# A gated delta rule kernel: log beta of the source token in the one decay exponent, instead of a second decay matrix

## The reference, cut to what matters

```
beta = sigmoid(hidden @ Wb.T)
g = -exp(A_log) * softplus(hidden @ Wa.T + dt_bias)
def step(S, inp):
    qt, kt, vt, gt, bt = inp
    S = S * exp(gt)                      # decay
    pred = einsum('bhk,bhkv->bhv', kt, S)
    dv = (vt - pred) * bt                # the write is scaled by beta
    S = S + einsum('bhk,bhv->bhkv', kt, dv)
    ot = einsum('bhk,bhkv->bhv', qt, S)
```

## Time and profile before

| | |
|---|---|
| runs | 1966.24, 1972.13, 1974.1 us; median 1972.13 us |
| span of the profiled execution | 1970.6 us (1.5 us less than the median of the runs) |
| TensorE matmul busy | 1809.7 us, 92% |
| VectorE busy | 1601.0 us, 81% |
| ScalarE busy | 1034.9 us, 53% |
| GpSimd busy | 414.1 us, 21% |
| chain that ended last, by engine | TensorE 76%, VectorE 10%, issue 9%, ScalarE 1% |
| TensorE clock, mean share granted | 0.944 |
| DMA | 13 GB/s on average |

### The profile page before, as it was taken

One profiled execution on the slowest core, in us unless ns is written; L12 is line 12 of the kernel. 1 busy time (PEld: TensorE's weight loads), 2 busy tenths in 40 slices (PEclk: granted clock), 3 DMA queues, 4 the chain that ended last, 5 costly groups with the idle time before them and its releaser, 6 DMA issues.

```text
span 1970.6 us, 102023 instructions
## 1 busy us (share of the span) xinstructions
PE 1809.7 (92%) x45376; PEld 1515.8 (77%) x45376; DVE 1601.0 (81%) x4326; ACT 1034.9 (53%) x1999; POOL 414.1 (21%) x325
## 2 busy tenths in 40 slices
PE   4689999999999999999999999999999999998886
PEld 3577787887878787878778877878887887787765
DVE  3777898888888888888988888899888889887631
ACT  3644555555555545555555555555555556554422
POOL 0212122222212222221222222122122221221200
PEclk8878999999999999999999999999999999998766
DMA  3000000000000000000000000000000000000000
GB/s 102 1 3 3 14 14 14 4 14 14 14 14 14 9 9 14 14 14 15 14 5 12 14 14 14 14 14 10 7 14 14 14 9 9 9 4 9 8 8 12
DMA packets 21447, 26.26 MB, mean 13 GB/s; under 512 B 2193, under 2 KB 20753, under 8 KB 21009
## 3 DMA queue, kind: packets, MB, share of 16 engines
q1 hardware_dynamic: 21008, 19.73, 3.0%
HBM read 11.33 MB, written 8.39 MB: 10 GB/s over the span
## 4 chain that ended last, share of the span: by engine, by line
PE 76%; DVE 10%; issue 9%; ACT 1%; DVEq 0%; POOL 0%; ACTq 0%; POOLq 0%
PE ps L239 36%; PE ps L221 15%; PE ps L230 9%; PE ps L214 4%; DVE CV L1107 3%; PE ps L411 2%; PE ps L363 2%; PE ps L589 2%; PE ps L579 2%; PE ps L598 2%; PE ps L207 2%; PE ps L381 1%; DVE XR L1384 1%; DVE eg L1364 1%; PE ps L472 1%
## 5 line engine op out<-in xcount | busy, mean ns | idle before, releaser
L1107 DVE SCALAR_TENSOR_TENSOR CV<-ps,cw,CV 128x256 f32<-128x256 f32 x576 | 250.5, 477 | 8.8 <-ACT CV L872 1.9
L239 PEld LDWEIGHTS ps<-QE,S 64*64 64x64 f32 x4096 | 212.4, 140 | 56.7 <-issue 55.2
L239 PE MATMUL ps<-QE,S 64*64 64x16 f32 x4096 | 254.9, 211 | 1.0 <-ACT S L673 1.0
L239 PE MATMUL ps<-WP,V 64*64 64x16 f32 x4096 | 252.5, 210 | 0.0
L239 PEld LDWEIGHTS ps<-WP,V 64*64 64x64 f32 x4096 | 213.4, 140 | 0.0
L239 PE MATMUL ps<-WP,KD 64*64 64x48 f32 x4096 | 144.6, 226 | 28.6 <-issue 26.8
L239 PEld LDWEIGHTS ps<-WP,KD 64*64 64x64 f32 x4096 | 134.4, 141 | 38.7 <-issue 37.4
L1007 POOL TENSOR_TENSOR XK<-XK 128x512 f32<-128x512 f32 x32 | 33.7, 1052 | 608.5 <-ACT XK L846 608.5
L1122 DVE TENSOR_TENSOR prod<-A,TZ 128x30 f32<-128x30 f32 (+7 forms) x480 | 141.4, 295 | 13.2
L239 PEld LDWEIGHTS ps<-SA,M 32*32 32x32 f32 x8192 | 93.2, 109 | 67.3 <-issue 40.5
L221 PE MATMUL ps<-w_r_ffn,XR 128*128 128x256 f32 x512 | 137.6, 416 | 6.7 <-DVE XR L1096 6.7
(11 more groups left out here) (156 smaller groups left out, 4019.8 us busy)
## 6 DMA issues: line engine op xcount, KB each, us to landing
X<-in_x SPq DMA_DIRECT2D x32, 256.0 KB, 2.7
out_x<-X SPq DMA_DIRECT2D x32, 256.0 KB, 2.1
w_r_ffn<-in_wT_r_ffn SPq DMA_DIRECT2D x1, 256.0 KB, 3.3
w_k_ffn<-in_wT_k_ffn SPq DMA_DIRECT2D x1, 256.0 KB, 3.6
w_v_ffn<-in_wT_v_ffn SPq DMA_DIRECT2D x1, 256.0 KB, 4.5
w_k<-in_wT_k SPq DMA_DIRECT2D x1, 256.0 KB, 4.5
w_q<-in_wT_q SPq DMA_DIRECT2D x1, 256.0 KB, 4.8
w_v<-in_wT_v SPq DMA_DIRECT2D x1, 256.0 KB, 5.1
```

The lines of the kernel that those rows point to most:

```text
L239: last = mm(ps[rows, o:o + n], stat[rows, pk].rearrange("p s c -> p (s c)"), mov[rows], **flags)
L1107: last = stt(d4[:, m], src, cw[:, i, m, tap:tap + 1], d4[:, m], ALU.mult, ALU.add)
```

## The change

Log beta of the source token j is put on the diagonal of `ST` before the running sums, so that the one exponent that `decay_steps` gives holds the decay from j to i and log beta of j. The one exponential `E` then carries beta wherever `EA` or `be` carried it:

- TensorE: `beta_in` (four 128x128 by 128x128 multiplications a group) is gone. `decay_steps` closes its sums itself.
- ScalarE: `beta_log` (128x512 copy) and `exp_a` (128x512 exponential) are gone.
- GpSimd: `b_diag` (128x512) is gone. `beta_diag` (128x512 product of -log beta and the diagonal mask, waits for `gb`) is new, and `stat1` has a second instruction, a 128x512 subtraction, that waits for the first one and for `beta_diag`.
- VectorE: `b_reduce` (a reduction of 128x512 and a 128x64 product) is gone. In `t_out0` and `t_out1` the product with `be` becomes a copy, and the product with `be2` becomes one with the mask `slot`; both have the shapes of before. `gram0` to `gram3` read `E` in place of `EA`.
- Waits: those on `ea`, `be`, `lb`, `bd` are gone or turned into waits on `e` and `ld`. The tiles `EA`, `LB`, `be`, `be2` are gone, `LD` is new.

```diff
@@ tensor
-                    last = mm(ps[:, o:o + P], ST[:, c0:c0 + P], cum_i, start=(ub == 0), stop=False, skip_group_check=True)
+                    last = mm(ps[:, o:o + P], ST[:, c0:c0 + P], cum_i, start=True, stop=True)
...
-            def beta_in(g):
-                pe.wait_ge(s["lb"], g + 1)
-                pe.wait_ge(s["e"], g + 1)
-                for ub in range(M * B):
-                    o, c0 = 4 * BANK + ub * P, (ub % B) * NH * C + ub // B * P
-                    last = mm(ps[:, o:o + P], LB[:, c0:c0 + P], ident, start=False, stop=(ub == M * B - 1), skip_group_check=True)
-                last.then_inc(s["ea_ps"], 1)
...
             def gram0(g):
                 pe.wait_ge(s["k_slots"], 4 * g + 4)
                 pe.wait_ge(s["qhat"], g + 1)
-                pe.wait_ge(s["ea"], g + 1)
+                pe.wait_ge(s["e"], g + 1)
@@ scalar
-            def beta_log(g):
-                act.wait_ge(s["gb"], g + 1)
-                if g:
-                    act.wait_ge(s["ea_ps"], g)
-                af(packs(LB[:]), along(cz[:, BH:2 * BH]), ACT.Copy, scale=-1.0).then_inc(s["lb"], 1)
...
-            def exp_a(g):
-                act.wait_ge(s["ea_ps"], g + 1)
-                if g:
-                    act.wait_ge(s["gram_used"], 4 * g)
-                    act.wait_ge(s["bd"], g)
-                af(EA[:], bank(4), ACT.Exp).then_inc(s["ea"], 1)
@@ gpsimd
-            def b_diag(g):
-                pool.wait_ge(s["ea"], g + 1)
-                pool.wait_ge(s["eg"], g + 1)
-                if g:
-                    pool.wait_ge(s["be"], g)
-                tt(packs(BD[:]), packs(EA[:]), over_packs(diag), ALU.mult).then_inc(s["bd"], 1)
...
+            def beta_diag(g):
+                pool.wait_ge(s["gb"], g + 1)
+                tt(packs(LD[:]), along(cz[:, BH:2 * BH]), over_packs(diag), ALU.mult).then_inc(s["ld"], 1)
+
             def stat1(g):
                 pool.wait_ge(s["gb_wide"], g + 1)
                 if g:
                     pool.wait_ge(s["d_ps"], g)
-                tt(packs(ST[:]), packs(GB[:]), vw(after_j, [0, BH], [1, C]), ALU.mult).then_inc(s["stat1"], 1)
+                own.done(tt(packs(ST[:]), packs(GB[:]), vw(after_j, [0, BH], [1, C]), ALU.mult))
+                pool.wait_ge(s["ld"], g + 1)
+                own.settle()
+                tt(ST[:], ST[:], LD[:], ALU.subtract).then_inc(s["stat1"], 1)
...
                 on(square3, g)
                 on(gate_norm, f)
                 on(q_decayed, e)
+                on(beta_diag, d)
                 on(stat1, d)
@@ vector
             def t_out0(g):
                 ve.wait_ge(s["t_ps"], 2 * g + 1)
-                ve.wait_ge(s["be"], g + 1)
...
                 own.done(tt(WP[g % 2][:, rows, 0:U].rearrange("p k (s c) -> p k s c", s=2),
-                            vw(src, [U, C], [0, 2], [1, C]), vw(be2[:, rows], [2, C], [1, 2], [0, C]), ALU.mult))
-                tt(WP[g % 2][:, rows, U:], src[:, :, C:U], along(be[:, rows]), ALU.mult).then_inc(s["wp"], 1)
+                            vw(src, [U, C], [0, 2], [1, C]), vw(slot, [0, C], [1, 2], [0, C]), ALU.mult))
+                nc.vector.tensor_copy(WP[g % 2][:, rows, U:], src[:, :, C:U]).then_inc(s["wp"], 1)
...
-                own.done(tt(packs(AT[:])[:, rows], src[:, :, 0:C], packs(EA[:])[:, rows], ALU.mult))
+                own.done(tt(packs(AT[:])[:, rows], src[:, :, 0:C], packs(E[:])[:, rows], ALU.mult))
...
-            def b_reduce(g):
-                ve.wait_ge(s["bd"], g + 1)
-                if g:
-                    ve.wait_ge(s["wp"], 2 * g)
-                chained(nc.vector.tensor_reduce(be[:], packs(BD[:]), AX_X, ALU.add))
-                tt(be2[:], along(be[:], 2), over_packs(slot), ALU.mult).then_inc(s["be"], 1)
```

More of the change, by code:

```diff
@@ L75, in macaron_kernel @@
         E = sb("E", [P, COLS])
-        EA = sb("EA", [P, COLS])
         EQ = sb("EQ", [P, COLS])
@@ L79, in macaron_kernel @@
         GD = sb("GD", [P, COLS])
-        BD = GD
         GI2 = sb("GI2", [P, PACKS, U])
@@ L84, in macaron_kernel @@
         A4 = sb("A4", [P, COLS])
-        LB = sb("LB", [P, COLS])
+        LD = sb("LD", [P, COLS])
         TZ = sb("TZ", [P, 2, 2, C, C])
@@ L119, in macaron_kernel @@
         names = ("first_in ffn_in mix_in x_in out_stored zeroed setup_act xt1_ps yt_ps xt3_ps k1_ps r1_ps v1_ps k3_ps r3_ps v3_ps "
-                 "q_ps k_ps v_ps g_ps ssk_ps ssq_ps oss_ps wo_ps eq_ps d_ps ea_ps hal1 hal3 haly rstd1 rstd2 rstd3 "
[3 rows of a table removed]
+                 "q_ps k_ps v_ps g_ps ssk_ps ssq_ps oss_ps wo_ps eq_ps d_ps hal1 hal3 haly rstd1 rstd2 rstd3 "
[3 rows of a table added]
                  "tapv gram_ps gram_used t_ps wp kd_ps mt b_ps o_ps ch_ps ch_s k_slots v_slots s_slots act_step "
-                 "vec_step").split()
+                 "vec_step pool_step").split()
         s = {n: sem(n) for n in names}
@@ L528, in ffn3_r @@
                     pe.wait_ge(s["gram_used"], min(4 * g + 9, 4 * GROUPS))
-                    pe.wait_ge(s["ea"], min(g + 3, GROUPS))
+                    pe.wait_ge(s["e"], min(g + 3, GROUPS))
                     pe.wait_ge(s["mt"], min(4 * g + 8, 4 * GROUPS))
@@ L632, in _ @@
                 on(chain, d, 1)
-                on(beta_in, c)
                 on(chain, d, 2)
@@ L943, in _ @@
                 on(norm1, b)
-                on(beta_log, d)
                 on(xt1, b)
@@ L952, in _ @@
                 on(norm3, f)
-                on(exp_a, d)
                 on(relu1, b)
@@ L986, in _ @@
             tt = nc.gpsimd.tensor_tensor
+            own = Steps(pool, s["pool_step"])
             def g_ident(g):
@@ L1053, in _ @@
                 on(g_ident, e)
-                on(b_diag, e)
                 on(square1, c)
@@ L1178, in soft_one @@
                     ve.wait_ge(s["gb"], g)
-                    ve.wait_ge(s["lb"], g)
+                    ve.wait_ge(s["ld"], g)
                 ts(uz[:], ez[:], 1.0, None, ALU.add).then_inc(s["uz"], 1)
@@ L1388, in gram0 @@
                 ve.wait_ge(s["gram_ps"], 4 * g + 1)
-                ve.wait_ge(s["ea"], g + 1)
                 ve.wait_ge(s["em"], g + 1)
@@ L1572, in _ @@
                 on(solve1, d)
-                on(b_reduce, d)
                 on(solve2, d)
```

2 lines of the change are left out of this document (removed), and 6 rows, old and new, of the table names.

## The result

| | before | after |
|---|---|---|
| median of 20 runs | 1972.69 us | 1985.01 us |
| lowest to highest | 1959.9 to 1983.1 | 1967.0 to 2000.5 |
| span of the profiled execution | 1970.6 us | 1987.4 us |
| TensorE clock in it, mean share granted | 0.944 | 0.931 |

The ratio after to before is 1.0064, with a 95% interval of 1.0044 to 1.0083: the kernel became 0.6% slower, where I had forecast 0.3% faster. The page of the kernel after shows what was expected in the busy times (GpSimd up from 414 to 437 us, the others down), and one thing that was not: the clock row.

The account below looks back on a forecast made before the run. TensorE's wait for `norm3` ahead of `turn3` was taken to cover `beta_in`'s saving. Terms 3.5 + 2.0 + 2.3 - 2.3 = 5.5 us less, so span 1965.1 and median 1966.6 us, 0.28% faster; range 1951 to 1990.

Parts of the forecast that it names:

- the one on the clock: New gap of 1.33 us ahead of `turn3`: judged nearer the 1.66 stop without a fall; no clock term in the sum.
- What bounds the kernel: TensorE at `turn3` waits for `norm3`, whose path does not pass through `beta_in`; `turn3` stays, gap grows 0.67 to 1.33.
- the term of 3.5 us: `chain 4` no longer set by VectorE's copy of `chain 3`: gain of 0.14 or 0.15 us in 24 groups.
- Rival A: `beta_in` on TensorE: the whole slot counts, 1.09 us in every group, 35 us gained, 1937 us; chance 0.06.
- Late groups: Groups where TensorE itself reaches `turn3` late: 0.57 us gained in three, 0.24 in a fourth, together 2.0 us.
- first and last groups: Gains of 1.1 us in the first group, 1.0 in the second, 0.2 in the last, together 2.3 us.
- GpSimd and `shift1`: GpSimd's longer work ahead of `stat1` holds `shift1` on VectorE, which ends 0.70 us later, as does `norm1`.
- the term of 2.3 us of loss: `turn1` waits for the later `norm1`: 0.32 us lost in 7 groups and 0.1 in one.
- rival D: VectorE ahead of `norm1`: `beta_diag` holds the statistics of `stats1`, `turn1` waits, 30 us lost, 1997 us; chance 0.08.
- The copies: VectorE's copy replacing the second product of `t_out0`: taken as 0, bounds -0.15 and 0 per copy.
- Rival B: Instructions reach TensorE sooner, relieving supply stops in rows of small instructions: 20 us more gained, 1945 us; chance 0.08.
- Rival C: Wider gap ahead of `turn3` makes TensorE's clock fall, 1.7 us each: 1987 us in half the groups, 2007 in all; chance 0.17.

Follow-up runs that it names:

- turn3_later: The kernel after with `turn3` moved behind `chain 3` and `gram0` on TensorE; 1981.35 us, ratio 1.0038 to the kernel before.
- after_again: The kernel after run once more, nothing changed; 1984.41 us, ratio 1.0050 to the kernel before.
- before_wide_gap: The kernel before, `beta_in` kept, with two extra activations delaying `norm3` to widen the gap ahead of `turn3`; 2011.23 us, ratio 1.0209.

## Why the prediction was wrong

The step that failed is the one on the clock: the sum holds no term for it, because I placed the new gap with the one that had no fall. The runs show falls behind that gap in 9 of 23 groups in one execution and 3 of 20 in another, and a mean clock of 0.934 instead of 0.943. The other terms first.

*What bounds the kernel*: right. `turn3` comes 7.31 us behind `decay_sums` in both kernels. The gaps are 0.36 and 1.33, in 23 groups where I counted 24 (in one of the 23 the second gap is 1.06, in one 1.58), and `chain 4` starts 0.07 ahead of the end of `gate`, 11.26 instead of 11.40 behind `decay_sums`. So the term of 3.5 us holds. Rival A is out.

*Late groups* (2.0) and *first and last groups* (2.3) can't be told apart from the falls in single traces. The one wait that can be followed, that for `T` in the first group, went from 10.3 to 9.5 us, as the 0.85 for `b_reduce` said. With the 3.5 the terms are 7.8, near the 6 to 7 us found at equal clock.

*GpSimd and `shift1`*: the mechanism was right, the size was not, and the term of 2.3 us of loss did not occur. `beta_diag` takes 1.05 us, not 1.29. In the tight groups `shift1` is held until the first product ends, as here (VectorE, GpSimd, ScalarE, TensorE):

```profile
817.88 0.81 DVE L1241 SCALAR_TENSOR_TENSOR nmr<-mv,rstd 128x2 f32<-128x2 f32 x1
...
817.37 1.29 POOL L999 TENSOR_TENSOR ST<-GB,msk 128x512 f32<-128x512 f32 x1
...
818.72 1.09 ACT L680 ACTIVATE XN<-X,nmr,rstd 128x256 f32<-128x256 f32 x2 [0.88 <-DVE nmr L1241]
...
819.87 0.33 PE L203 MATMUL ps<-cst,XN 128*128 128x128 f32 x1
```

`shift1` ends 2.41 behind `gates`, against 2.04 before: 0.37 later, not 0.70. `norm1` ends 0.06 ahead of `turn1`, which starts 1.89 behind the first product of `k_proj` in these groups, against 1.85 in the tight groups of before: it loses 0.04 at most where I took 0.32. The statistics took 0.41 us beside GpSimd and without it, so rival D is out. The copies took 0.414, as the products did: 0, as taken. The subtraction took 1.283 (1.28 taken).

*Rival B*: TensorE's gaps further than 34 us behind `decay_sums`, where the stops of supply stand, sum to some 51 us in before and 54 in after (those above 0.1 us). Not relieved.

*Rival C is what happened, and this is the step that failed.* I had two gaps with a clock behind them, 2.22 with a fall and 1.66 without, placed the new one with the second, put the clock at nothing in the sum, and gave C 0.17. Two rows can't bear that: 1.66 without a fall in one group says nothing of 23 groups. In after the gap of 1.33 brought a fall in nine groups and none in the others, in another execution in three of twenty: its length alone does not tell whether the clock falls. Even behind the 0.82 in `turn3_later` it fell in three groups. The cost per fall (1.7) and the point of turning (four groups) were right: nine falls are 15 us. In the profiled execution the sum is -3.5 - 2.0 - 2.3 + 0 + 15 = +7, and the falls at the two other places are 20.5 us longer than before, at most 10 us more. That makes 17, and the spans differ by 16.8. For the 28 groups alone it is -3.5 - 2.0 + 15 + 10, or some 20, and they are 21.3 longer. What stands at the two other places I can't assign to the change: in `after_again` these places had 58.0 us, in before 61.4, in after 81.9. In after six of the nine groups with a fall behind `turn3` have another some 40 us behind `decay_sums`, and five of the other 19; in `before_wide_gap` it is two of six and eight of 22, so whether one fall draws the next stays open. The mean of all runs (clock 0.934 against 0.943) says that more is lost than gained, but not at which place.

What I did not see at all is how deep the cover is. I wrote that up to 1.09 us a group would come through if the path to `norm3` were shorter. Behind it stood the copy of `chain 3`, and behind that VectorE's part of `gram0`; only with all three out of the way came 0.66 through. Most of the rest of the 1.09 is the wait of 0.36 ahead of `chain 2`, which this order still has.

## What to carry to other kernels

Work taken out of a busy engine where it next waits for another engine turns into idle time, and on TensorE idle time has a price of its own: look at the granted clock behind each gap that grows, over many groups and several executions, and give even one that is shorter than a gap without a fall a real chance. Fill the gap or, better, cut it up or take away the wait; a product that looks useless may be holding the clock. Before judging a saving, follow the wait behind the wait: the same edit cost 12 us in one order and gave 21 in another. And look at the first and last groups too when an order is changed for the common one.

## What was unexpected of the hardware

Constant products that take 1.09 us of TensorE in every group made the kernel 15 us faster (1969.8 against 1984.4). Behind a gap of 2.9 us the clock stayed at its lower level (1.2 GHz) for up to 34 us of work without a pause, in seven of 24 falls for over 30, where behind 1.33 it was back after 3.4. And a VectorE instruction of two columns took 1.60 us as soon as it was the first to meet GpSimd's running `g_ident`. The falls need no transposes right behind the gap: those of 0.82 and 2.9 us stood ahead of `gate` and `ffn3_r`. Whether transposes make a fall more likely was not tried.
